# Products of zeros behind both attentions, and all variances ahead of the logits, in a one-core transformer kernel

## The reference, cut to what matters

```
h = tokenizer(x)                              # patches, three norms, silu
h = concat([h, txt])                          # 269 tokens a batch
h = h + nystrom_attention(layernorm(h))       # 8 heads, 128 landmarks, 6 steps of a pseudo-inverse
h = h + mixture_of_8(layernorm(h))            # router: top 2 of 8, each expert 64 -> 256 -> 64, gelu
h = h + distance_attention(layernorm(h))      # exp(-gamma * max(|q|^2 + |k|^2 - 2qk, 0)) @ v, 8 heads
h = h + mixture_of_4(layernorm(h))            # shared MLP plus top 2 of 4 experts
layernorm(h) = (h - mean(h)) / sqrt(var(h) + eps)
```

## Time and profile before

| | |
|---|---|
| median of 3 runs | 730.26 us (728.4, 730.26, 735.58) |
| the profiled execution, its own time | 736.04 us |
| its span, first to last instruction | 734.2 us |
| TensorE busy | 681.5 us, 93% of the span |
| VectorE, ScalarE, GpSimd busy | 413.5, 377.6, 229.7 us |
| TensorE's mean granted clock | 0.939 of full |

### The profile page before, as it was taken

How to read it: one execution, slowest core, us unless ns; L and a number is a source line. 1 busy time by engine, 2 the same in 40 slices (tenths; PEclk the granted TensorE clock), 3 DMA queues, 4 the chain that set the end, 5 groups by cost and what they waited for, 6 DMA issues and landing times. The chain is left out here.

```text
span 734.2 us, 15178 instructions
## 1 busy us (share of the span) xinstructions
PE 681.5 (93%) x6033; PEld 527.5 (72%) x6033; DVE 413.5 (56%) x843; ACT 377.6 (51%) x1035; POOL 229.7 (31%) x204
## 2 busy tenths in 40 slices
PE   9887898999999999999889999869999999989896
PEld 5676798988989898988785555557666666647555
DVE  3457347667575767674525333426777777764322
ACT  4656447565655647473246555335555455544531
POOL 4155325343544344444300434023222222201001
PEclk9997699999999999999958999957999999996999
DMA  8200000000000000000000000000000000000000
GB/s 267 99 3 1 1 1 3 2 1 2 1 2 2 2 1 3 2 1 2 1 1 1 1 1 1 1 1 1 1 1 1 1 2 1 1 1 1 1 15 17
DMA packets 5214, 8.23 MB, mean 11 GB/s; under 512 B 3608, under 2 KB 4120, under 8 KB 4760
## 3 DMA queue, kind: packets, MB, share of 16 engines
q1 hardware_dynamic: 4552, 7.20, 3.1%
q10 hardware_dynamic: 592, 0.07, 0.1%
HBM read 6.71 MB, written 0.55 MB: 10 GB/s over the span
## 5 line engine op out<-in xcount | busy, mean ns | idle before, releaser
L977 POOL TENSOR_TENSOR STD<-STD,NN 91x492 f32<-91x492 f32 (+1 forms) x96 | 104.0, 1101 | 149.2 <-DVE NN L1106 78.7
L677 PE MATMUL PS<-ST 128*91 128x123 f32 x768 | 92.9, 272 | 4.8 <-DVE ST L1112 4.6
L1106 DVE SCALAR_TENSOR_TENSOR NN<-ST,PS 91x492 f32<-91x492 f32 x96 | 62.9, 661 | 56.3 <-PE PS L677 56.3
L677 PE MATMUL PS<-NN 128*91 128x123 f32 (+1 forms) x768 | 89.6, 268 | 3.2 <-DVE NN L1106 3.2
L677 PEld LDWEIGHTS PS<-ST 128*91 128x91 f32 x768 | 83.5, 159 | 11.0 <-DVE ST L1112 7.1
L677 PEld LDWEIGHTS PS<-NN 128*91 128x91 f32 x768 | 82.2, 160 | 10.4 <-DVE NN L1106 6.4
L1746 PE MATMUL PS<-QR,KA 128*128 128x270 f32 x256 | 72.2, 413 | 0.0
L895 ACT ACTIVATE STD<-ST 91x492 f32<-91x492 f32 (+1 forms) x96 | 51.6, 569 | 39.6 <-DVE ST L1112 39.6
L1860 DVE TENSOR_SCALAR CL<-PS,K 128x270 f32<-128x270 f32 x144 | 65.7, 496 | 9.8 <-PE PS L1746 4.5
L1112 DVE SCALAR_TENSOR_TENSOR ST<-PS,STD 91x492 f32<-91x492 f32 (+1 forms) x96 | 55.9, 599 | 22.1 <-POOL STD L977 12.4
L1801 ACT ACTIVATE EX<-CL,NG 128x540 f32<-128x540 f32 x64 | 46.7, 741 | 32.8 <-DVE CL L1860 32.7
(11 more groups left out here) (326 smaller groups left out, 1250.5 us busy)
## 6 DMA issues: line engine op xcount, KB each, us to landing
TP<-taps SPq DMA_DIRECT2D x1, 1204.0 KB, 16.1
MA<-mat SPq DMA_DIRECT2D x1, 1120.0 KB, 7.5
MF<-mat SPq DMA_DIRECT2D x1, 1024.0 KB, 12.6
WI<-wide SPq DMA_DIRECT2D x1, 902.0 KB, 9.0
CO<-const SPq DMA_DIRECT2D x1, 512.0 KB, 15.7
MQ<-mat SPq DMA_DIRECT2D x1, 512.0 KB, 16.4
out<-OS SPq DMA_DIRECT2D x8, 45.0 KB
XA<-xpatch SPq DMA_DIRECT2D x1, 256.0 KB, 2.8
```

The source lines that it names most:

```text
L677: last = nc.tensor.matmul(PS[0:NL, PINV + q, h % 4 * SW + c0:(h % 4 + 1) * SW], x[:, h, 0:NL], x[:, h, c0:SW], start=True, stop=True)
L977: nc.gpsimd.tensor_tensor(TD[:, 4 * q:4 * q + 4, c0:SW], SA[:, 4 * q:4 * q + 4, c0:SW], NN[0:NL, 4 * q:4 * q + 4, c0:SW], ALU.subtract).th ...
L1106: v.scalar_tensor_tensor(out=NN[0:NL, own, :], in0=ST[0:NL, b % 2, own, :], scalar=N_S, in1=heads4(PS[0:NL, PINV + q, 0:4 * SW]), op0=ALU. ...
```

## The change

`spin` and ZK are moved out of block 1, so that all blocks can use them, and `spin` gets the bank as an argument. (Its branch for `low` is called by nobody.) Two products of zeros stand between the last `attend` and the last `out_proj`, eight behind that `out_proj`, and four behind the last `weigh` of block 4. The wait in front of the four is for copies that were made long before. In `norm_pe` the loop is split: the variances of all four pairs, then the logits of all four pairs. This concerns block 3 and block 5.

```diff
+        ZK = sb("ZK", [128, 512], F32R)
...
+        def spin(n, bank=7, low=0):
+
+            for _ in range(n):
+                if low:
...
+                else:
+                    nc.tensor.matmul(PS[:, bank, :], ZK[:, 0:128], ZK[:, :], start=True, stop=True)
...
-        ZK = ts("ZK", [128, 512], F32R)
         HC = B * NI // 2
-        SPIN = 7
...
-                def spin(n):
-
-                    for _ in range(n):
-                        nc.tensor.matmul(PS[:, SPIN, :], ZK[:, 0:128], ZK[:, :], start=True, stop=True)
...
+        SPARE = 2
...
                 attend(B - 1, 0)
                 attend(B - 1, 1)
+                spin(2, SPARE)
                 out_proj(B - 1)
+                spin(8, SPARE)
...
             for p in range(BP):
                 pe.wait_ge(sem(tag + "_squared"), p + 1)
                 variances(p, VARS, KT * p).then_inc(sem(tag + "_var"), 1)
+            for p in range(BP):
                 pe.wait_ge(sem(tag + "_kept"), p + 1)
                 logits(p, weights, n).then_inc(sem(tag + "_logit"), 1)
...
                 batches(pe, body)
+                need(pe, ("d_vm", atb("d_vm", B // 2 - 1, 1, 4, 4)))
+                spin(4, 5)
```

More of the change, by code:

```diff
@@ L162, in program @@
         AA = fs("AA", [128, B, H, SW])
+        def spin(n, bank=7, low=0):
+            for _ in range(n):
+                if low:
+                    nc.tensor.matmul(PS[low:128, bank, 0:256], ZK[:, 0:128 - low].bitcast(F32), ZK[:, 0:256].bitcast(F32),
+                                     start=True, stop=True)
+                else:
+                    nc.tensor.matmul(PS[:, bank, :], ZK[:, 0:128], ZK[:, :], start=True, stop=True)
         def col(t, c, p=128, n=1):
```

## The result

In the runs compared, the changed kernel takes 728.29 us in the median (12 runs, 725.11 to 738.11), the kernel before 732.60 (12 runs, 728.40 to 736.17). The ratio is **0.9944, with an interval of 0.9917 to 0.9971**: 4.1 us faster, between 2.1 and 6.1. Two more comparisons of the same code gave 0.9944 and 0.9940. The forecast was 724, 6.6 us of gain, from a median of 730.26 of three runs; twelve put that median at 732.6.

What follows compares the result with a forecast made beforehand. It took TensorE, full but at half clock after blocks 2 and 4, as the bound. Block 3 gains 4.6 us (5.2 + 0.3 − 0.9) and block 5 2.0: 730.3 − 6.6 = 723.7, said as 724; range 719 to 728, 717 to 732 for 8 in 10.

Steps and rivals of the forecast that it cites:

- What the products do to the clock, and where it falls: Blocks 3 and 5: clock high when the centring starts, then falling in the variances, logits or spread.
- The two products: Ahead of block 2's last output product: at most 0.58 us, covered by ScalarE's copy, so they cost nothing.
- The eight: Behind block 2's last output product: 2.04 us of products, so block 3 starts 0.9 us later.
- The four: Behind block 4: 1.06 us of products, covered by VectorE's two additions, so cost 0.
- The order: In the norms, roots run beside the four groups of logits; the idle 0.61 us before the spread goes.
- Block 3, up to the spread: Block 3's norm: 11.8 us becomes 5.7 at the high clock, gain 4.3 to 6.1, taken as 5.2.
- Block 5: Block 5's norm and spread: 8.3 us before, gain 2.0 us, between 0.8 and 5.1.
- The sum: Blocks 3 and 5 together: 6.6 us gained, giving 724 against the median of 730.3.
- The chances: Whole kernel: faster by over 1% 0.36, within 1% 0.58, slower by over 1% 0.06; the forecast itself 0.62.
- The clock held throughout: Rival, chance 0.11: clock stays high through both norms, 14.8 us gained, 715.5.
- Not held at all: Rival, chance 0.15: clock falls at the block ends as before, 0.3 us gained, 730.
- Moved, not shortened: Rival, chance 0.12: half-rate stretch begins inside the norm and lasts as long, 6.5 us slower, 736.8.

Runs made afterwards that it cites:

- zeros only: The changed kernel with variances and logits alternating as before, all fourteen products of zeros kept: 735.42 us, 1.0028 against the kernel before.
- The second and third traces: The kernel before, unedited, profiled twice more: spans 731.3 and 728.7 us, ratios 0.9981 and 0.9987 against itself.
- The fourth and fifth trace: The changed kernel plus five products of zeros before each of block 5's first three final products, traced twice: medians 726.38 and 727.27 us, 0.9908 and 0.9939.
- final zeros: Five products of zeros before each of block 5's first three final products; added to the changed kernel 0.9908 and 0.9939, to the kernel before 0.9985.

## Why the prediction was right and wrong

*What the products do to the clock, and where it falls.* Right in all traces of the changed kernel: high through the centring (2.06 us in both blocks), fallen within the norm. The sign it named, a fall between the second variance and the spread, is right for block 3 in the first two traces (1.3 and 0.3 us ahead of the spread). In the third the fall comes 0.2 us into the spread, as these windows show, and in block 5 it comes 0.9 to 1.1 us into it in all three:

```profile
367.52:373.20 5.68, 5.68 (x56) 5.34 (x57) 2.21 (x5) 4.10 (x9) 0.96 (x1) 1.00 0.01 3
373.20:376.20 3.00, 3.00 (x17) 3.00 (x17) 2.08 (x6) 2.95 (x6) 0.00 (x0) 0.54 0.00 0
```

Its reason, that narrow products do not keep the clock, is not shown to be the whole: with a product of 512 columns ahead of each group the clock fell in block 5 all the same.

*The two products.* 0 forecast and 0 measured: from the last products of `attend` to the output product it is 1.06 us before and 1.07 after, though the two took 0.73 us and not 0.58. *The eight.* Forecast +0.9 at the barrier, measured 0.99 (2.83 to 3.82). *The four.* 0 forecast; they end at 653.34, 0.18 us behind VectorE, and the block starts 0.81 us after them: right within 0.2.

*The order.* The gap of 0.6 us in front of the spread went, and the roots run during the logits; zeros only has one again (1.07 and 0.76 us). Right.

*Block 3, up to the spread.* **This term failed.** It took "Before: 368.38 to 380.17, 11.8 us" from one execution as what before costs, and 5.2 us as the gain. The second and third traces have 8.63 and 8.64, so that the term measures 8.64 − 5.94 = 2.7 us (5.94 is the mean of the changed kernel's three). In them the clock came back near the centring's end for the variances and logits, which the prediction had seen in block 5 and did not consider for block 3. It had noted that the profiled execution was 5.8 us over the median, and did not use it. The gain of block 3, forecast 4.6, is 5.2 against the first trace, but 24.1 − 22.3 = 1.8 us against the other two. The mechanism stands, the size doesn't.

*Block 5.* Forecast 2.0, measured 22.7 − 19.2 = 3.5. The term took off 0.9 us for a fall among the logits, which came later in all three traces (norm 5.69), and counted 0.3 for a spread partly at full speed, which gave 0.7 in the first. The fourth and fifth trace have 19.18 and 20.45, so that the gain in one execution can be 2.2.

*The sum.* 1.8 + 3.5 = 5.3 us by the traces (5.2 with the traces that have final zeros), 4.1 (2.1 to 6.1) by the runs, forecast 6.6. What lies between 5.3 and 4.1 is inside the interval; late dips in some executions could fill it, which is not shown. The low stretches of block 2 move the start of block 3 by 4 us from one execution to the next (the last output product starts at 365.42, 367.70 and 363.68 in the three traces of the changed kernel); nothing in the change touches them.

*The chances.* Most was put on within 1%, and 0.56% faster is within; that it can nevertheless be told from no change is owed to the number of runs, and to a bound of 1% that was drawn from the scatter of three. The forecast of 724 was 4.3 us low: 2.3 of it is the base, as much again the gain (6.6 against 4.3 between the medians), less 0.3 of rounding up. 728.29 lies inside the wide range, 717 to 732, but just outside the forecast's own, 719 to 728, and the wide one had been drawn to reach into the rivals.

*The rivals.* The clock held throughout did not come true: the clock fell with TensorE busy 4.10 of 4.10 us in block 3's norm, and its last idle time before, 1.11 us at the barrier, had ended 5 us earlier. The Trainium skill (TensorE: Matmul & The Clock Gate, HAM oscillation) puts such a fall down to waits in which TensorE idles; this row goes against that. Nor would it have been worth 14.8 us: held by force in block 3 up to 381.1, it gave back about 2 us from the spread on, where the rival counted 2.5 + 1.5, since the spread waits for VectorE; and the products that held it cost 2.05. Not held at all: excluded by the centring. Moved, not shortened: not in block 3, where the low stretch is 10.2 us in place of 13.7 to 23.9. But in kind it is what ate the gain of zeros only, as late dips in block 5, a place that the prediction never priced. That a changed arrival can cost 6.5 us far behind the change was missing from the list.

## What to carry to other kernels

A clock dip that one trace shows at a place needs a second and third trace before it is priced: here the same code had 11.8 us once and 8.6 three times. Idle products paid in this kernel where the engine would wait in front of wide, dependent work, up to the moment at which the others reach the barrier; beyond it they cost their own time. Look at the waits behind them too, since holding the clock at one place changed where it fell at the next. Take stretches between fixed instructions, not totals, to judge a piece.

## What the runs showed of the hardware

- Final products of 64 columns behind a wait of 1.65 us let the clock fall in the traces of two variants and not in those of the changed kernel, with the same code there; an end of 50.7 us becomes 57.2. Five products of zeros in the wait took this away in the variant in which it was tried (50.83).
- Inside a norm, one zero product of 512 columns ahead of each six narrow ones held the clock at 1.00 for 11.6 us in block 3 and not in block 5 of the same execution (0.83 over 9.3 us, then 0.50). The logits have 8 columns there in place of 16, so the code is not quite the same; what made the difference is open.
- In block 3 of before the clock came back near the end of a centring that ran at half (TensorE busy 3.65 of 3.70 us) when the centring started 0.1 to 0.6 us after the fall (three traces), and did not when it started 0.8 us after (one). From the first centring to the first spread it was 8.6 us in the three, 11.8 in the one.
